# Conditioned residual pair kernel: 8 KB load rows and 16 KB store rows in two rings, and evictions of 2048 columns

## The chip, the cores and the metric

One core of a Trainium2 chip runs the kernel. The metric is the device time of one launch in microseconds (us); the time of a kernel is the median of its runs. Engines are called as the profile calls them: PE is TensorE (PEld its weight loads), DVE is VectorE, ACT is ScalarE, POOL is GpSimd, SP is SyncE. ACTq and SPq are the instruction queues of ACT and SP, from which they issue transfers.

## The reference

```python
def reference(x, itok_B_0_15, itok_B_0_31, L0_cond_weights, L1_cond_weights, L1_cond_biases):
    # x: (128, 128, 2048) f32; conditions: (128,) int32
    W = L0_cond_weights[itok_B_0_15]               # 16 maps of 128x128
    x = x + einsum('bct,bcd->bdt', x, W)
    w = L1_cond_weights[itok_B_0_31]               # 32 maps of 128x128
    b = L1_cond_biases[itok_B_0_31]
    return x + einsum('bct,bcd->bdt', x, w) + transpose(b, (0, 2, 1))
```

For a sample this is (I + W1)(I + W0) applied to a 128x2048 matrix, plus a bias per row. Input and output are 134 MB each.

## The kernel before

The kernel first makes one 128x128 map for each sample, the product of the two maps with the identity added to each, and then multiplies the sample by it. It works on 64 pairs of samples (`PAIRS`), q = 0 to 63.

**Layout.** A pair is 2 MB. It is loaded in one transfer of 128 rows of 16 KB: partition k*64+i holds channels 2i and 2i+1 of sample k of the pair (`x_pairs`, lines 34 on). So sample 0 lies on partitions 0 to 63 and sample 1 on 64 to 127, and u = 0, 1 names the even and the odd channels. There are 8 slots (`xt`, `SLOTS`). The result is written back into the slot it was read from, and stored from there in rows of 16 KB.

**SP** (lines 101 to 110) loads the weights and then the pairs. From the ninth pair on it waits, before it loads into a slot, until the store from that slot has landed (`stored`).

**POOL** (lines 124 to 138) adds the identity to the two maps of each sample (lines 136 and 137), up to two pairs ahead (`map0T`, `map1`).

**PE** (lines 150 to 209). `combine` (line 154) multiplies the maps, in two matmuls of 256 columns for a pair, into the last 512 columns of `acc1`; ACT copies the halves that are wanted into `both`. `term` (line 159) is a matmul of 512 columns that contracts only 64 partitions: the channels of one parity of one sample. Sample 0 goes to `acc0`, sample 1 to `acc1`, each four PSUM banks of 512 columns, and each bank takes two terms (u = 0 and 1). There are 16 terms in a pair, written in turn for the two samples. A float32 matmul is two instructions in the profile (MATMUL x2048 for 1024 terms). Halves of the accumulators (columns 0 to 1023 and 1024 to 2047) are handed over on their own: `lo_done` after the first, `hi_done` after the second.

**DVE** (lines 222 to 233) evicts sample 0 with the bias, four instructions of 64x1024 per pair (lines 224, 226), and **ACT** (lines 242 to 265) sample 1 in the same way (line 251). ACT also copies the combined map of the next pair (lines 246, 247) between its evictions, and issues the pair's store (line 265) once all four parts are out.

The order of PE within a pair is written out by hand (`pair`):

```python
pe.wait_ge(x_loaded[slot], loads)      # then 8 terms on columns 0..1023
pe.wait_ge(hi_out[prev], outs_before)  # the pair before is out of the upper half
combine(next, next_maps)               # then 5 terms on columns 1024..2047
pe.wait_ge(both_ready[next], next_both)
                                       # 2 terms
pe.wait_ge(lo_out[slot], outs)         # last term
```

Eight pairs are unrolled at the start, eight form the body of a loop, and eight are unrolled at the end.

Of the kernel before, what the change touches and what calls it, by code (L numbers as in the profile page):

```python
# [5 lines left out]
def conditioned_residual_kernel(  # L6
# [16 lines left out]
    B, C, T = x.shape  # L23
# [3 lines left out]
    HALF = T // 2  # L27
    SLOTS = 8
    PAIRS = B // 2
    TURNS = PAIRS // SLOTS  # L30
# [4 lines left out]
    x_pairs = x.rearrange("(q k) (i u) t -> q (k i) (u t)", k=2, u=2)  # L35
# [3 lines left out]
    with ctx:  # L39
# [20 lines left out]
        map0T = sb("map0T", [C, 2, 2, 2, HC])  # L60
# [22 lines left out]
        maps_ready = [sem(f"maps_ready{s}") for s in range(SLOTS)]  # L83
        combined = sem("combined")
        both_ready = [sem(f"both_ready{s}") for s in range(SLOTS)]
        lo_done0 = sem("lo_done0")
        lo_done1 = sem("lo_done1")
        hi_done0 = sem("hi_done0")
        hi_done1 = sem("hi_done1")

        lo_out = [sem(f"lo_out{s}") for s in range(SLOTS)]
        hi_out = [sem(f"hi_out{s}") for s in range(SLOTS)]
        x_loaded = [sem(f"x_loaded{q}") for q in range(SLOTS)]
        stored = [sem(f"stored{q}") for q in range(SLOTS)]

        w0T_v = w0T_sb[:, :, :].rearrange("p s (i u) -> p s u i", u=2)
# [5 lines left out]
        @block.sync  # L102
        def _(sp):
            sp.dma_start(w0T_sb[:, :, :], w0T).then_inc(w0_loaded, LOAD)
            sp.dma_start(w1_sb[:, :, :], w1).then_inc(w1_loaded, LOAD)
            for q in range(PAIRS):
                slot = q % SLOTS
                if q >= SLOTS:
                    sp.wait_ge(stored[slot], LOAD * (q // SLOTS))
                sp.dma_start(xt[:, slot, :], x_pairs[q, :, :]).then_inc(x_loaded[slot], LOAD)  # L110

        @block.gpsimd
        def _(pool):
# [9 lines left out]
            GROUP = 16  # L123
            for b in range(B):
                if b % GROUP == 0:
                    _, i0 = nc.values_load_multi_w_load_instructions(  # L126
                        cond_sb[0:1, 0, b:b + GROUP], engines=[POOL], min_val=0, max_val=S0 - 1,
                        skip_runtime_bounds_check_because="conditions index the maps")
                    _, i1 = nc.values_load_multi_w_load_instructions(  # L129
                        cond_sb[0:1, 1, b:b + GROUP], engines=[POOL], min_val=0, max_val=S1 - 1,  # L130
                        skip_runtime_bounds_check_because="conditions index the maps")
# [4 lines left out]
                nc.gpsimd.tensor_tensor(map0T[:, q % 2, :, k, :], w0T_v[:, bass.ds(i0[b % GROUP], 1), :, :], ident_v, ALU.add)  # L136
                nc.gpsimd.tensor_tensor(map1[:, q % 2, k, :, :], w1_v[:, bass.ds(i1[b % GROUP], 1), :, :], ident_v,  # L137
                                        ALU.add).then_inc(maps_ready[q % SLOTS], 1)

        @block.tensor  # L140
        def _(pe):
# [8 lines left out]
            def combine(slot, ready):  # L150

                pe.wait_ge(maps_ready[slot], ready)
                for u in range(2):
                    last = nc.tensor.matmul(acc1[:, CB + u * 2 * C:CB + (u + 1) * 2 * C],  # L154
                                            map0T[:, slot % 2, u, :, :], map1[:, slot % 2, :, :, :], start=True, stop=True)
                last.then_inc(combined, 1)

            def term(acc, k, u, buf, slot, j):
                return nc.tensor.matmul(acc[:, j * CHUNK:(j + 1) * CHUNK], both[k * HC:(k + 1) * HC, buf, u, :],  # L159
                                        xt[k * HC:(k + 1) * HC, slot, u * T + j * CHUNK:u * T + (j + 1) * CHUNK],  # L160
                                        start=u == 0, stop=u == 1)

            def pair(slot, outs, outs_before, next_maps, next_both, loads, begins, ends):

                buf = slot % 2
                prev, next = (slot - 1) % SLOTS, (slot + 1) % SLOTS
                if begins:
                    pe.wait_ge(both_ready[0], 1)

                pe.wait_ge(x_loaded[slot], loads)  # L170
                term(acc0, 0, 0, buf, slot, 0)
                term(acc1, 1, 0, buf, slot, 0)
                term(acc0, 0, 1, buf, slot, 0)
                term(acc1, 1, 1, buf, slot, 0)
                term(acc0, 0, 0, buf, slot, 1)
                term(acc1, 1, 0, buf, slot, 1)
                term(acc0, 0, 1, buf, slot, 1).then_inc(lo_done0, 1)
                term(acc1, 1, 1, buf, slot, 1).then_inc(lo_done1, 1)
                if not begins:
                    pe.wait_ge(hi_out[prev], outs_before)  # L180
                if not ends:
                    combine(next, next_maps)
                term(acc0, 0, 0, buf, slot, 2)
                term(acc1, 1, 0, buf, slot, 2)
                term(acc0, 0, 1, buf, slot, 2)
                term(acc1, 1, 1, buf, slot, 2)
                term(acc0, 0, 0, buf, slot, 3)
                if not ends:

                    pe.wait_ge(both_ready[next], next_both)  # L190
                term(acc1, 1, 0, buf, slot, 3)
                term(acc0, 0, 1, buf, slot, 3).then_inc(hi_done0, 1)
                if not ends:
                    pe.wait_ge(lo_out[slot], outs)
                term(acc1, 1, 1, buf, slot, 3).then_inc(hi_done1, 1)

            def group(twos, twos_before, twos_after, after, now, loads, begins, ends):

                for s in range(SLOTS):
                    wraps = s == SLOTS - 1  # L200
                    pair(s, twos, twos_before if s == 0 else twos, twos_after if wraps else twos,
                         after if wraps else now, loads, begins and s == 0, ends and wraps)

            pe.wait_ge(bias_ready, 1)
            combine(0, 2)
            group(2, 0, 4, 2, 1, LOAD, True, False)
            with pe.Fori(2, TURNS) as now:
                group(now * 2, now * 2 - 2, now * 2 + 2, now + 1, now, now * LOAD, False, False)
            group(2 * TURNS, 2 * TURNS - 2, 2 * TURNS + 2, TURNS + 1, TURNS, TURNS * LOAD, False, True)

        @block.vector
        def _(dve):
# [9 lines left out]
            def even_out(q, a):  # L222

                nc.vector.tensor_scalar(xt[0:HC, q % SLOTS, a:a + HALF], acc0[0:HC, a:a + HALF],  # L224
                                        bias_of[0:HC, 2 * q:2 * q + 1], None, ALU.add)
                return nc.vector.tensor_scalar(xt[0:HC, q % SLOTS, T + a:T + a + HALF], acc0[HC:C, a:a + HALF],  # L226
                                               bias_of[HC:C, 2 * q:2 * q + 1], None, ALU.add)

            for q in range(PAIRS):
                dve.wait_ge(lo_done0, q + 1)  # L230
                even_out(q, 0).then_inc(lo_out[q % SLOTS], 1)
                dve.wait_ge(hi_done0, q + 1)
                even_out(q, HALF).then_inc(hi_out[q % SLOTS], 1)

        @block.scalar
        def _(act):
# [5 lines left out]
            def copy_maps(q):  # L242

                act.wait_ge(combined, q + 1)
                crossed = acc1[:, CB:T].rearrange("p (u k c) -> p u k c", u=2, k=2)
                nc.scalar.activation(both[0:HC, q % 2, :, :], crossed[0:HC, :, 0, :], ACT.Identity)  # L246
                nc.scalar.activation(both[HC:C, q % 2, :, :], crossed[HC:C, :, 1, :], ACT.Identity).then_inc(both_ready[q % SLOTS], 1)  # L247

            def odd_out(q, v, a):

                return nc.scalar.activation(xt[HC:C, q % SLOTS, v * T + a:v * T + a + HALF], acc1[v * HC:(v + 1) * HC, a:a + HALF],  # L251
# [3 lines left out]
            for q in range(PAIRS):  # L255
                act.wait_ge(lo_done1, q + 1)
                odd_out(q, 0, 0)
                if q < PAIRS - 1:
                    copy_maps(q + 1)
                odd_out(q, 1, 0).then_inc(lo_out[q % SLOTS], 1)  # L260
                act.wait_ge(hi_done1, q + 1)
                odd_out(q, 0, HALF)
                odd_out(q, 1, HALF).then_inc(hi_out[q % SLOTS], 1)
                act.wait_ge(hi_out[q % SLOTS], 2 * (q // SLOTS + 1))
                act.dma_start(out_pairs[q, :, :], xt[:, q % SLOTS, :]).then_inc(stored[q % SLOTS], LOAD)
            for q in range(SLOTS):
                act.wait_ge(stored[q], LOAD * TURNS)
# [27 lines left out]
```

## Time and profile before

| what | value |
|---|---|
| median of 3 runs | 642.13 us (642.07 to 642.19) |
| the profiled execution: its own time | 642.29 us |
| its span | 640.4 us |
| PE busy | 538.4 us (84%) |
| DVE busy | 329.2 us (51%) |
| ACT busy | 333.5 us (52%) |
| POOL busy | 124.2 us (19%) |
| moved by DMA | 271.82 MB, mean 424 GB/s |

The span is the time between the first and the last event of the execution; its own time is 1.9 us longer. Shares are of the span. Busy time says how full an engine is on average and not who waits for whom: that is in the waits, the chain that ended last and the timeline. There are 16 DMA engines; a queue's share is the time of its packets over 16 times the span. A packet is one row of a transfer as one engine moves it.

### The profile page before, as it was taken

Reading aid. Unit: us, or ns where it says so; the run is one execution under the profiler, and the core shown is the slowest. Engines: PE = TensorE matmul, PEld = TensorE weight load, DVE = VectorE, ACT = ScalarE, POOL = GpSimd, SP = SyncE. Lnnn points to the kernel's source line nnn. Section 1 sums busy time; section 2 is a strip of 40 time slices with the busy share of each in tenths; the row PEclk is TensorE's granted clock in tenths of the full one; section 3 lists DMA queues with packets and bytes.
Section 4 is the critical chain, followed back from the end, with each engine's and each line's share of the span. In section 5 each row is a group of like instructions: output and inputs, shape, how many; then the busy total and the mean of one; then the engine's idle time right before and its main releaser. Section 6 shows DMA issues by size and latency. Waiting matters only on the chain.

```text
span 640.4 us, 6061 instructions
## 1 busy us (share of the span) xinstructions
PE 538.4 (84%) x2308; PEld 234.3 (37%) x2308; DVE 329.2 (51%) x259; ACT 333.5 (52%) x385; POOL 124.2 (19%) x263
## 2 busy tenths in 40 slices
PE   1899999999889889888898898888988988988860
PEld 0344444444334333333333333333333333433320
DVE  0266666666554455455545554555455445545550
ACT  0366666666555465455554654555555545545550
POOL 2322222222122122121221221211212212112000
PEclk9999999999999999999999999999999999999995
DMA  8999999999999999999999999999999999999996
GB/s 363 433 415 427 431 432 426 431 433 428 432 433 427 432 434 427 431 434 427 432 434 426 433 435 426 432 433 428 433 431 428 433 431 430 431 433 428 434 429 262
DMA packets 18931, 271.82 MB, mean 424 GB/s; under 512 B 2241, under 2 KB 2274, under 8 KB 2274
## 3 DMA queue, kind: packets, MB, share of 16 engines
q1 hardware_dynamic: 9504, 137.37, 50.3%
q10 hardware_dynamic: 9410, 134.26, 49.0%
q8 instruction: 7, 0.11, 0.1%
q14 instruction: 10, 0.08, 0.0%
HBM read 137.40 MB, written 134.22 MB: 424 GB/s over the span
## 4 chain that ended last, share of the span: by engine, by line
DMA 64%; PE 29%; DVE 3%; POOLq 0%; ACT 0%; issue 0%; DVEq 0%; POOL 0%; SPq 0%; ACTq 0%
DMA out_dram<-xt 40%; PE acc L159 25%; DMA xt<-in_x_dram 23%; PE acc L154 4%; DMA w_sb<-in_w_dram 1%; DVE xt L224 1%; DVE xt L226 1%; DVEq L39 0%; ACT L246 0%; POOLq L126 0%; POOLq L129 0%; POOL map0T L136 0%; POOL map L137 0%; ACT both L247 0%; ACT both L246 0%
## 5 line engine op out<-in xcount | busy, mean ns | idle before, releaser
L159 PE MATMUL acc<-xt,both 64*128 64x512 f32 x2048 | 472.5, 603 | 67.9 <-DMA xt<-in_x_dram 65.7
L251 ACT ACTIVATE xt<-acc,bias_of 64x1024 f32<-64x1024 f32 x256 | 283.7, 1108 | 270.1 <-PE acc L159 267.7
L159 PEld LDWEIGHTS acc<-xt,both 64*128 64x128 f32 x2048 | 189.8, 188 | 319.0 <-issue 211.5
L224 DVE TENSOR_SCALAR xt<-acc,bias_of 64x1024 f32<-64x1024 f32 x128 | 163.3, 1276 | 278.2 <-PE acc L159 278.2
L226 DVE TENSOR_SCALAR xt<-acc,bias_of 64x1024 f32<-64x1024 f32 x128 | 165.0, 1289 | 1.9
L136 POOL TENSOR_TENSOR map0T<-w0T_sb,ident 128x128 f32<-128x128 f32 x128 | 65.6, 513 | 465.8 <-PE acc L154 454.0
L154 PE MATMUL acc<-map,map0T 128*128 128x256 f32 x256 | 73.3, 409 | 1.2 <-POOL map L137 1.2
L137 POOL TENSOR_TENSOR map<-w_sb,ident 128x128 f32<-128x128 f32 x128 | 65.7, 513 | 0.0
L154 PEld LDWEIGHTS acc<-map,map0T 128*128 128x128 f32 x256 | 43.9, 191 | 53.0 <-issue 36.7
L247 ACT ACTIVATE both<-acc 64x256 f32<-64x256 f32 x64 | 24.3, 380 | 0.8
L246 ACT ACTIVATE both<-acc 64x256 f32<-64x256 f32 x64 | 24.2, 377 | 0.8
L246 ACT ACT_TABLE_LOAD x1 | 1.3, 1283 | 17.4 <-PE acc L154 17.4
L145 PE MATMUL acc<-ident,bias_sb 128*32 128x128 f32 x2 | 0.6, 418 | 10.8 <-DMA bias_sb<-in_bias_dram 10.8
L215 DVE TENSOR_TENSOR onehot<-cond_rep,row 32x128 f32<-32x128 int32 x1 | 0.3, 279 | 12.6 <-DMA cond_rep<-in_conds_dram 12.6
L145 PEld LDWEIGHTS acc<-ident,bias_sb 128*32 128x32 f32 x2 | 0.2, 142 | 10.8 <-DMA bias_sb<-in_bias_dram 10.8
L148 PE MATMUL acc<-onehot,biasT 32*128 32x128 f32 x2 | 0.8, 481 | 1.9 <-DVE biasT L217 1.9
L148 PEld LDWEIGHTS acc<-onehot,biasT 32*128 32x128 f32 x2 | 0.5, 304 | 2.3 <-DVE onehot L215 2.3
L219 DVE COPY bias_of<-acc 128x128 f32<-128x128 f32 x1 | 0.3, 292 | 0.9 <-PE acc L148 0.9
L217 DVE COPY biasT<-acc 32x128 f32<-32x128 f32 x1 | 0.3, 278 | 0.0
L117 POOL TENSOR_SCALAR_AFFINE_SELECT ident<-ident 128x128 f32<-128x128 f32 x1 | 0.3, 283 | 0.0
L114 POOL MEMSET ident<- 128x128 f32 x1 | 0.2, 204 | 0.3 <-POOLq L284 0.3
L115 POOL IOTA row<- 32x128 int32 x1 | 0.2, 224 | 0.0
(4 smaller groups left out, 0.4 us busy)
## 6 DMA issues: line engine op xcount, KB each, us to landing
xt<-in_x_dram SPq DMA_DIRECT2D x64, 2048.0 KB, 24.5
out_dram<-xt ACTq DMA_DIRECT2D x64, 2048.0 KB, 42.9
w_sb<-in_w_dram SPq DMA_DIRECT2D x1, 2048.0 KB, 9.4
w0T_sb<-in_w0T_dram SPq DMA_DIRECT2D x1, 1024.0 KB, 4.8
cond_sb<-in_conds_dram ACTq DMA_DIRECT2D x1, 1.0 KB
bias_sb<-in_bias_dram ACTq DMA_DIRECT2D x1, 16.0 KB, 9.4
cond_rep<-in_conds_dram ACTq DMA_DIRECT2D x1, 16.0 KB, 10.8
```

Source lines behind the costliest of these rows:

```text
L117: nc.gpsimd.affine_select(out=ident[:, :], in_=ident[:, :], compare_op=ALU.not_equal, fill=1.0, base=0, pattern=[[-1, C]], channel_multipl ...
L136: nc.gpsimd.tensor_tensor(map0T[:, q % 2, :, k, :], w0T_v[:, bass.ds(i0[b % GROUP], 1), :, :], ident_v, ALU.add)
L137: nc.gpsimd.tensor_tensor(map1[:, q % 2, k, :, :], w1_v[:, bass.ds(i1[b % GROUP], 1), :, :], ident_v, ALU.add).then_inc(maps_ready[q % SLO ...
L145: nc.tensor.matmul(acc0[0:S1, 0:C], bias_sb[:, :], ident[:, :], start=True, stop=True).then_inc(turned, 1)
L148: nc.tensor.matmul(acc1[:, 0:B], biasT[:, :, :], onehot[:, :], start=True, stop=True).then_inc(picked, 1)
L154: last = nc.tensor.matmul(acc1[:, CB + u * 2 * C:CB + (u + 1) * 2 * C], map0T[:, slot % 2, u, :, :], map1[:, slot % 2, :, :, :], start=Tru ...
L159: return nc.tensor.matmul(acc[:, j * CHUNK:(j + 1) * CHUNK], both[k * HC:(k + 1) * HC, buf, u, :], xt[k * HC:(k + 1) * HC, slot, u * T + j ...
L224: nc.vector.tensor_scalar(xt[0:HC, q % SLOTS, a:a + HALF], acc0[0:HC, a:a + HALF], bias_of[0:HC, 2 * q:2 * q + 1], None, ALU.add)
L226: return nc.vector.tensor_scalar(xt[0:HC, q % SLOTS, T + a:T + a + HALF], acc0[HC:C, a:a + HALF], bias_of[HC:C, 2 * q:2 * q + 1], None, AL ...
L246: nc.scalar.activation(both[0:HC, q % 2, :, :], crossed[0:HC, :, 0, :], ACT.Identity)
L247: nc.scalar.activation(both[HC:C, q % 2, :, :], crossed[HC:C, :, 1, :], ACT.Identity).then_inc(both_ready[q % SLOTS], 1)
L251: return nc.scalar.activation(xt[HC:C, q % SLOTS, v * T + a:v * T + a + HALF], acc1[v * HC:(v + 1) * HC, a:a + HALF], ACT.Identity, bias=b ...
```

## The change

The sample is no longer folded by parity. A load puts channel c of both samples of a pair on partition c, as two rows of 8 KB (256 rows per pair), into a ring of 6 slots of its own (`xin`). Results go to a second ring of 4 slots (`xout`) in the old folded layout, and stores keep their rows of 16 KB.

- SP waits, before it loads pair q, for `done1` of pair q-6, that is for PE to have read the slot, and no longer for a store.
- A term contracts all 128 partitions, so a pair takes 8 terms and not 16. `combine` multiplies only the two products that are wanted, in two matmuls of 128 columns, and ACT copies them in one instruction of 128x256.
- PE does the four terms of sample 0 (`acc0`), hands over the whole accumulator (`done0`), then combines for the next pair and does the four terms of sample 1 (`done1`).
- DVE and ACT each evict a sample in two instructions of 64x2048.
- PE waits for the store of pair q-4 to have landed before its second term of pair q, and for the load of pair q+1 before the second term of sample 1 of pair q.
- ACT waits for DVE's result before its second eviction of the pair.
- The unrolled groups are of 12, the loop body is of 12 and runs three times, then 12 and 4 more are unrolled.

```diff
-    x_pairs = x.rearrange("(q k) (i u) t -> q (k i) (u t)", k=2, u=2)
+    x_pairs = x.rearrange("(q k) c t -> c q k t", k=2)
     out_pairs = out.rearrange("(q k) (i u) t -> q (k i) (u t)", k=2, u=2)
...
-        xt = sb("xt", [C, SLOTS, 2 * T])
+        xin = sb("xin", [C, IN, 2, T])
+        xout = sb("xout", [C, OUT, 2 * T])
...
-                if q >= SLOTS:
-                    sp.wait_ge(stored[slot], LOAD * (q // SLOTS))
-                sp.dma_start(xt[:, slot, :], x_pairs[q, :, :]).then_inc(x_loaded[slot], LOAD)
+                if q >= IN:
+                    sp.wait_ge(done1, q - IN + 1)
+                sp.dma_start(xin[:, q % IN, :, :], x_pairs[:, q, :, :]).then_inc(x_loaded[q % GROUP], LOAD)
...
+            def combine(k, p):
+                return nc.tensor.matmul(acc1[:, CB + k * C:CB + (k + 1) * C], map0T[:, p % 2, k, :], map1[:, p % 2, k, :, :],
+                                        start=True, stop=True)
+            def term(acc, k, p, j):
+                return nc.tensor.matmul(acc[:, j * CHUNK:(j + 1) * CHUNK], both[:, p % 2, k, :],
+                                        xin[:, p % IN, k, j * CHUNK:(j + 1) * CHUNK], start=True, stop=True)
+            def pair(p, turn_before, turn_after, loads, loads_after, stores, begins, ends):
+                prev, next = (p - 1) % GROUP, (p + 1) % GROUP
+                if begins and p == 0:
+                    pe.wait_ge(both_ready[0], 1)
+                    pe.wait_ge(x_loaded[0], loads)
+                else:
+                    pe.wait_ge(out0[prev], turn_before)
+                term(acc0, 0, p, 0)
+                if not (begins and p < OUT):
+                    pe.wait_ge(stored[(p - OUT) % GROUP], stores)
+                term(acc0, 0, p, 1)
+                if not ends:
+                    pe.wait_ge(maps_ready[next], turn_after)
+                term(acc0, 0, p, 2)
+                term(acc0, 0, p, 3).then_inc(done0, 1)
+                if not (begins and p == 0):
+                    pe.wait_ge(out1[prev], turn_before)
+                if not ends:
+                    combine(0, p + 1)
+                    combine(1, p + 1).then_inc(combined, 1)
+                term(acc1, 1, p, 0)
+                if not ends:
+                    pe.wait_ge(x_loaded[next], loads_after)
+                term(acc1, 1, p, 1)
+                term(acc1, 1, p, 2)
+                if not ends:
+                    pe.wait_ge(both_ready[next], turn_after)
+                term(acc1, 1, p, 3).then_inc(done1, 1)
...
+                dve.wait_ge(done0, q + 1)
+                nc.vector.tensor_scalar(xout[0:HC, q % OUT, 0:T], acc0[0:HC, :], bias_of[0:HC, 2 * q:2 * q + 1], None, ALU.add)
+                nc.vector.tensor_scalar(xout[0:HC, q % OUT, T:2 * T], acc0[HC:C, :], bias_of[HC:C, 2 * q:2 * q + 1], None,
+                                        ALU.add).then_inc(out0[q % GROUP], 1)
...
+                nc.scalar.activation(both[:, q % 2, :, :], acc1[:, CB:CB + 2 * C], ACT.Identity).then_inc(both_ready[q % GROUP], 1)
+            def odd_out(q, v):
+                return nc.scalar.activation(xout[HC:C, q % OUT, v * T:(v + 1) * T], acc1[v * HC:(v + 1) * HC, :],
                                             ACT.Identity, bias=bias_of[v * HC:(v + 1) * HC, 2 * q + 1:2 * q + 2])
...
             for q in range(PAIRS):
                 if q < PAIRS - 1:
                     copy_maps(q + 1)
+                act.wait_ge(done1, q + 1)
+                odd_out(q, 0)
+                act.wait_ge(out0[q % GROUP], q // GROUP + 1)
+                odd_out(q, 1).then_inc(out1[q % GROUP], 1)
+                act.wait_ge(out1[q % GROUP], q // GROUP + 1)
+                act.dma_start(out_pairs[q, :, :], xout[:, q % OUT, :]).then_inc(stored[q % GROUP], LOAD)
```

## Rows read from the trace of the kernel before

**Rows 1.** The page's span in 40 slices: granted PE clock, DMA busy share and rate.
```profile
PEclk9999999999999999999999999999999999999995
DMA  8999999999999999999999999999999999999996
GB/s 363 433 415 427 431 432 426 431 433 428 432 433 427 432 434 427 431 434 427 432 434 426 433 435 426 432 433 428 433 431 428 433 431 430 431 433 428 434 429 262
```

**Rows 2.** The page's DMA queues: packets, MB, share of 16 engines (q1 loads, q10 stores).
```profile
q1 hardware_dynamic: 9504, 137.37, 50.3%
q10 hardware_dynamic: 9410, 134.26, 49.0%
q8 instruction: 7, 0.11, 0.1%
```

**Rows 3.** Waits of SP's queue: us in total, times, longest us.
```profile
SPq L110 <- DMA out_dram<-xt: 563.2, 56, 42.8
```

**Rows 4.** The chain that ended last, in order of time: start us, us, what.
```profile
132.97 7.07 PE acc L159 x32
141.10 7.07 PE acc L159 x32
...
155.50 40.01 DMA out_dram<-xt
195.53 24.59 DMA xt<-in_x_dram
```

**Rows 5.** Timeline of PE, two pairs in mid-span: start us, us, instructions, idle before.
```profile
406.82 3.70 PE L159 MATMUL acc<-xt,both 64*128 64x512 f32 x16 [1.43 <-DMA xt<-in_x_dram]
...
416.62 3.70 PE L159 MATMUL acc<-xt,both 64*128 64x512 f32 x16 [1.40 <-DMA xt<-in_x_dram]
```

**Rows 6.** The page's DMA issues: KB each, median us from issue to landing.
```profile
xt<-in_x_dram SPq DMA_DIRECT2D x64, 2048.0 KB, 24.5
out_dram<-xt ACTq DMA_DIRECT2D x64, 2048.0 KB, 42.9
...
w0T_sb<-in_w0T_dram SPq DMA_DIRECT2D x1, 1024.0 KB, 4.8
...
bias_sb<-in_bias_dram ACTq DMA_DIRECT2D x1, 16.0 KB, 9.4
```

**Rows 7.** End of the timeline: the last pair on PE, and the issue of its store.
```profile
613.06 7.14 PE L159 MATMUL acc<-xt,both 64*128 64x512 f32 x32 [1.41 <-DMA xt<-in_x_dram]
...
622.84 0.34 ACTq L265 DMA_DIRECT2D out_dram<-xt  x1
```

**Rows 8.** DMA queues from 634.7 to 639.4 us: packets, MB, share of 16 engines.
```profile
q10 hardware_dynamic: 10, 0.11, 5.7%
```

**Rows 9.** DMA queue from 3 to 4.2 us, when only rows of 8 KB move.
```profile
q1 hardware_dynamic: 62, 0.51, 100.9%
```

**Rows 10.** DMA queues from 6 to 9 us: 16 KB rows on q1, 128-byte rows on q10.
```profile
q1 hardware_dynamic: 80, 1.31, 101.9%
q10 hardware_dynamic: 80, 0.01, 2.2%
```

**Rows 11.** DMA queue q10 from 10 to 30 us, packets of 512 bytes and less.
```profile
q10 hardware_dynamic: 66, 0.02, 0.4%
```

**Rows 12.** The page's groups: busy us, mean ns of one, idle before and releaser.
```profile
L159 PE MATMUL acc<-xt,both 64*128 64x512 f32 x2048 | 472.5, 603 | 67.9 <-DMA xt<-in_x_dram 65.7
L251 ACT ACTIVATE xt<-acc,bias_of 64x1024 f32<-64x1024 f32 x256 | 283.7, 1108 | 270.1 <-PE acc L159 267.7
...
L224 DVE TENSOR_SCALAR xt<-acc,bias_of 64x1024 f32<-64x1024 f32 x128 | 163.3, 1276 | 278.2 <-PE acc L159 278.2
...
L154 PE MATMUL acc<-map,map0T 128*128 128x256 f32 x256 | 73.3, 409 | 1.2 <-POOL map L137 1.2
...
L247 ACT ACTIVATE both<-acc 64x256 f32<-64x256 f32 x64 | 24.3, 380 | 0.8
...
L219 DVE COPY bias_of<-acc 128x128 f32<-128x128 f32 x1 | 0.3, 292 | 0.9 <-PE acc L148 0.9
```

More of the change, by code:

```diff
@@ L82, in conditioned_residual_kernel @@
         bias_ready = sem("bias_ready")
-        maps_ready = [sem(f"maps_ready{s}") for s in range(SLOTS)]
         combined = sem("combined")
[L85 to L96, printed above, removed]
+        done0 = sem("done0")
+        done1 = sem("done1")
+        x_loaded = [sem(f"x_loaded{p}") for p in range(GROUP)]
+        stored = [sem(f"stored{p}") for p in range(GROUP)]
+        maps_ready = [sem(f"maps_ready{p}") for p in range(GROUP)]
+        both_ready = [sem(f"both_ready{p}") for p in range(GROUP)]
+        out0 = [sem(f"out0_{p}") for p in range(GROUP)]
+        out1 = [sem(f"out1_{p}") for p in range(GROUP)]
         w1_v = w1_sb[:, :, :].rearrange("p s (i u) -> p s u i", u=2)
@@ L148, in _ @@
             nc.tensor.matmul(acc1[:, 0:B], biasT[:, :, :], onehot[:, :], start=True, stop=True).then_inc(picked, 1)
[L150 to L167, printed above, removed]
-                    pe.wait_ge(both_ready[0], 1)
[L170 to L180, printed above, removed]
-                if not ends:
[L182 to L187, printed above, removed]
@@ L188, in pair @@
                 if not ends:
-                    pe.wait_ge(both_ready[next], next_both)
-                term(acc1, 1, 0, buf, slot, 3)
-                term(acc0, 0, 1, buf, slot, 3).then_inc(hi_done0, 1)
+                    combine(0, p + 1)
+                    combine(1, p + 1).then_inc(combined, 1)
+                term(acc1, 1, p, 0)
                 if not ends:
[L194 to L202, printed above, removed]
@@ new lines, in pair, with group @@
+                if not ends:
+                    pe.wait_ge(both_ready[next], turn_after)
+                term(acc1, 1, p, 3).then_inc(done1, 1)
+            def group(places, now, before, after, loads, loads_before, loads_after, begins, ends):
+                for p in range(places):
+                    wraps = p == GROUP - 1
+                    pair(p, before if p == 0 else now, after if wraps else now, loads, loads_after if wraps else loads,
+                         loads_before if p < OUT else loads, begins, ends and p == places - 1)
@@ new lines, in _ @@
+            pe.wait_ge(bias_ready, 1)
+            pe.wait_ge(maps_ready[0], 1)
+            combine(0, 0)
+            combine(1, 0).then_inc(combined, 1)
+            group(GROUP, 1, 0, 2, LOAD, 0, 2 * LOAD, True, False)
+            with pe.Fori(2, FULL) as now:
+                group(GROUP, now, now - 1, now + 1, now * LOAD, now * LOAD - LOAD, now * LOAD + LOAD, False, False)
+            group(GROUP, FULL, FULL - 1, FULL + 1, FULL * LOAD, (FULL - 1) * LOAD, (FULL + 1) * LOAD, False, False)
```

57 lines of the change are left out of this document (16 added, 41 removed).

## The prediction

> **What bounds the kernel now.** I read the slices first. The DMA engines are full from the second slice to the last but one, at about 431 GB/s [rows 1], while TensorE's granted clock is at its upper level (2.4 GHz) up to the last slice. The two queues share that time almost evenly, 50.3% and 49.0%, so packets fill 99.3% of sixteen engines' span [rows 2]. The waits and the chain say the same of the order of work: SP, which only loads, stands for 563.2 us behind stores that have not landed [rows 3]. The chain consists of PE work in the first part, with pairs 8.13 us apart (132.97, 141.10), and from 155 us on it goes round through a store of 40.0 us, a load of 24.6 us and a short piece of compute [rows 4]. In mid-span PE starts pairs 9.80 us apart and each time has waited 1.4 us for the load [rows 5]. So compute is done in 8.1 us and DMA sets 9.8.
>
> The pitch can be taken apart. Sixteen-KB packets take 0.611 us: 101.9% of 16 x 3 us over 80 packets [rows 10]. A pair is 8 such packets per engine to load and 8 to store, 16 x 0.611 = 9.78 us. That is the whole pitch, so the engines are never idle in mid-span.
>
> The end matters too. The last load lands just before 613.06 us, and the span ends 27.3 us later [rows 7]. From 634.7 to 639.4 us the packets fill 5.7% of sixteen engines, 0.91 of one engine: a single engine is about 5 us behind the other fifteen [rows 8]. I take it to be the one that also fetches instructions (7 packets of 16 KB on a queue of their own) [rows 2]. What it still has at 613 us is a backlog of stores: at 42.9 us from issue to landing over a pitch of 9.8, 4.4 stores are under way [rows 5, 6]; about 0.9 of these is already moved, and two more are to come, 5.5 x 8 x 0.611 = 26.9 us of packets. It has that to do and finishes about 1 us before the span ends. So even in the tail the slowest DMA engine never stands idle, and compute of the last pair (9.8 us from 613.06 to its store's issue at 622.84) is hidden under stores. The kernel's time is this engine's packets plus some 3 us. A change can then move the time in only two ways: by the time of the packets, or by opening a hole in the slowest engine's work.
>
> **The packets (paid in full).** Loads go from 8 rows of 16 KB to 16 rows of 8 KB per engine and pair, 64 x 8 = 512 more packets on each engine. The 8 KB rows of the first weights took 100.9% of 16 x 1.2 us over 62 packets, 0.312 us each [rows 9]; two are 0.013 us more than one of 16 KB, 512 x 0.013 = 6.6 us. That window is short and its edges cut packets, so it is the upper end. Another bound: 66 packets of at most 512 bytes took 0.4% of 16 x 20 us, 1.28 us; their 0.02 MB at 27 GB/s per engine are 0.74 us, which leaves 8 ns per packet that no byte explains [rows 11]. That is 512 x 0.008 = 4.1 us. The lower end is nothing: a fixed part might hide under the other queue's packet. I take 4.1 us, which comes from the most packets, in a mixed stretch like the one that counts. The Trainium skill (DMA: Bandwidth & Descriptors, "Why small descriptors are slow") charges each DMA operation 32 bytes of descriptor metadata: 8192 more of them would be 0.26 MB or, as an estimate, 0.6 us, and a sum by it would come 3.5 us lower; rows 11 show more than that per packet.
>
> **How the engines share between the two queues.** From 6 to 9 us, q10 moved 80 packets of about 128 bytes and q1 moved 80 of 16 KB [rows 10]: packets alternate one for one, whatever their size. So a 16 KB bias load took 9.4 us [rows 6]. Now both queues have 16 KB packets and share evenly; after the change a load packet is half as long, so stores get two thirds of an engine whenever both have work. A store of 4.9 us of packets then needs 4.9 / (2/3) = 7.4 us, less than the 9.85 us between stores, and its backlog drains. What piles up are loads: with 6 slots, pair q+6 is issued when q has been read, so four to five loads are always queued and the engines stay busy. Steady pitch: 9.80 + 8 x 0.008 = 9.86 us.
>
> **Compute (hidden).** Eight terms are 16 instructions of 512 columns. Before, 32 such in two concurrent rows take 7.07 us [rows 4], 0.43 us a step, so four terms are 8 x 0.43 = 3.4 us and eight 6.9. Combining goes from four instructions in 1.15 us (73.3/64) to four of half the columns, 0.6 to 1.15 [rows 12]; I take 0.7. DVE: 128 columns take 0.292 us and 1024 take 1.276, so 1.1 ns per column and 2048 take 2.40, two are 4.8 us; ACT: 256 columns 0.380, 1024 columns 1.108, so 2048 take 2.08, two are 4.2 us [rows 12]. (Upper ends: twice the present instruction, 5.1 and 4.4 us.) Two circles limit a pair: 3.4 of sample 0's terms, then DVE's 4.8, together 8.3 with hand-overs; and 4.2 of ACT, 0.7 combine, 3.4 terms, 8.4. Both lie under 9.86 with 1.4 us to spare. The new wait for the next load stands in mid-pair: after it landed (L), PE still does three terms, 2.7 us with fill; ACT evicts until L+6.9; then combine and one term, until L+8.5. That too fits. POOL's additions keep their number and size and wait for PE as now; SP's wait moves to `done1` and has nothing but loads behind it. ACT's wait for DVE holds its second eviction, the store and the next map copy, but DVE is done 4.8 us after sample 0, before sample 1's terms plus one eviction (3.4 + 0.7 + 2.1). PE's wait for the store of four pairs ago comes some 25 us after its issue, against 7.4 us of packets and 2 of latency. None of this is seen while loads are the last to come; if that cover went, each microsecond of pitch over 9.86 would cost up to 64.
>
> **The tail (opened).** Count from L, the landing of the last load. Store 61 was issued at L-9.86+7.0 = L-2.9. From issue to first packet I take 1.2 us and from last packet to landing 1.0: a 1 MB load landed in 4.8 us [rows 6] of which 8 x 0.312 = 2.5 are packets. So store 61 runs from L-1.7, has done 1.1 us of its 4.9 by L, and ends at L+3.8. Store 62 is issued at L+7.0 (2.7 + 4.2 + 0.1), runs from L+8.2 to L+13.1: a hole of 4.4 us. Pair 63's sample 1 starts on PE when ACT has left, L+6.9, takes 3.6 with fill, then ACT 4.2 and 0.1: issue at L+14.8, packets from L+16.0 to L+20.9: a hole of 2.9. The span ends at about L+21.9. Both holes together, 7.3 us, are time in which the slowest engine has nothing, where it now has none. Ends: 5.5 us (faster evictions, quicker first packet) to 9.
>
> **The sum.** 640.4 + 4.1 + 7.3 = 651.8 us of span. The profiled execution took 642.29 for its span of 640.4, and the median of the runs shown is 642.13; added to the median, 642.1 + 11.4 = 653.5 us. At the start nothing moves: six loads fill the engines until about 40 us, and the seventh is issued at about 30.
>
> **Rivals.**
> *Shares go by bytes (0.15), the one that can end on the other side.* If the two queues keep equal halves of the engines, stores drain in 9.8 us, no faster than they come; the backlog built while compute sets the pace (8.4 against 9.8 per pair over some twenty pairs) stays, up to the 25 us that PE's wait for `stored` lets pass. Then 2.3 stores are left at L, 11 us, and no hole opens. Only the packets' term is left: 642.1 + 4.1 = 646.2, from 642.1 to 648.7. It ends as no change or better if the fixed part is under 2.5 ns a packet. Rows 10 speak against it. The Trainium skill (DMA: Bandwidth & Descriptors, "Queues, rings and completion order") has an engine drain a packet of about 9 to 17 descriptors from one ring before it switches; that would be a whole transfer's 16 small rows against 8 large ones, equal bytes, and hence this rival's time. By that rule, rows 10 should have shown runs of packets and not equal counts.
> *The slowest engine is relieved (0.04).* It is 4.7 us behind the rest [rows 8]. If the new code fetched fewer instructions and the backlog also stayed, the time would come to 638 to 641. But the unrolled pairs rise from 24 to 40 while the instructions per pair halve.
> *Compute becomes the bound (0.05).* If evictions of 2048 columns across four banks cost 0.8 us more each than I take, the circle passes 9.86; at 10.2 us per pair it adds some 20 us, 674. PE is less full, 7.6 of 9.86 us; would its clock fall to the lower level, terms would take 13.7 us and the time pass 900. Gaps of 1.4 us leave it high now [rows 1, 5].
> *The two rows of a partition lie 1 MB apart in memory and read slower (0.03).* Each tenth on the loads' packets is 1024 x 0.031 = 32 us.
> *My forecast: 0.73.*
>
> **How the numbers follow.** A measurement of this kernel can tell about 0.2%, 1.3 us. Faster: 0.04 from the relieved engine and 0.02 of the byte shares; same: 0.04 of the byte shares; slower: all else, 0.90. The forecast's own ends are 642.1 + 5.5 = 647.6 and 642.1 + 6.6 + 9 = 657.7. The range reaches down into the byte shares: 645.0 to 657.5.
>
> **What would show it.** Per step: q1 with about 17,700 packets and a share some 0.6 points up; pitch of 9.86 us; stores landing in 10 us and not 42.9, loads in 40 or more; SP waiting for PE; the last load landing about 22 us before the end, and a hole in the rate between L+4 and L+8 and again near L+13 to L+16. It is wrong if stores still take over 25 us to land (shares by bytes), if PE waits longest for DVE or ACT in mid-span (compute bound), or if the pitch is not 9.8 to 9.9.

## The result, and the profile after

The changed kernel takes 647.67 us, the median of 5 runs (647.26 to 649.29), against 642.11 for the kernel before in the same series. The ratio is 1.0087, with a 95% interval of 1.0076 to 1.0098. It is 5.6 us slower. The forecast was slower by 11.4 us, from 645.0 to 657.5. The sign is right and the time lies in the range, but the size was forecast at twice what was measured.

The page of the changed kernel: its span, the slices (clock, DMA share, rate), the queues, and the two large groups of transfers with KB each and median us to landing. They answer to [rows 1, 2, 6].

```profile
span 645.5 us, 3621 instructions
...
PEclk9999999999999999999999999999999999999998
DMA  8999999999999999999999999999999999999986
GB/s 362 428 409 429 429 427 428 429 437 429 423 427 429 429 428 432 432 423 429 430 428 434 430 425 430 429 428 439 424 431 424 426 433 429 425 431 427 427 366 260
...
q1 hardware_dynamic: 17696, 137.37, 50.5%
q10 hardware_dynamic: 9410, 134.26, 48.6%
q8 instruction: 6, 0.10, 0.1%
q14 instruction: 7, 0.06, 0.0%
...
xin<-in_x_dram SPq DMA_DIRECT2D x64, 2048.0 KB, 46.0
out_dram<-xout ACTq DMA_DIRECT2D x64, 2048.0 KB, 11.5
```

DMA still fills the span, but the last slice but one is thinner: 366 GB/s, where there were 429. Stores now land in 11.5 us and not in 42.9, loads in 46.0 and not in 24.5: the queue that used to be long is short, and the other way round.

The page's groups of the changed kernel (busy us, mean ns, idle before) answer to [rows 12].

```profile
L155 PE MATMUL acc<-xin,both 128*128 128x512 f32 x1024 | 469.2, 601 | 84.1 <-DMA xin<-in_x_dram 75.2
L240 ACT ACTIVATE xout<-acc,bias_of 64x2048 f32<-64x2048 f32 x128 | 251.1, 1962 | 287.0 <-PE acc L155 286.2
L222 DVE TENSOR_SCALAR xout<-acc,bias_of 64x2048 f32<-64x2048 f32 x64 | 149.9, 2343 | 320.1 <-PE acc L155 320.1
...
L151 PE MATMUL acc<-map,map0T 128*128 128x128 f32 x256 | 45.2, 300 | 34.6 <-ACT xout L240 32.6
```

Evictions of 2048 columns cost 2.34 us on DVE and 1.96 on ACT (forecast 2.40 and 2.08), combining 45.2/64 = 0.71 us a pair (0.7). PE still waits longest for loads.

The chain that ended last in the changed kernel (start us, us, what) shows the pitch: five pairs lie between two of its PE pieces.

```profile
134.66 2.85 PE acc L155 x6
...
183.68 2.86 PE acc L155 x6
...
232.43 2.85 PE acc L155 x6
...
427.82 2.86 PE acc L155 x6
...
624.13 2.86 PE acc L155 x6
```

From 232.43 to 427.82 are 20 pairs, 9.77 us each; from there to 624.13 another 20, 9.82 each. Forecast was 9.86 throughout, and 9.77 lies outside the 9.8 to 9.9 that were to confirm it. Before the change it was 9.82: from 406.82 [rows 5] to 613.06 [rows 7] are 21 pairs. The 9.80 of the prediction is a single step of it.

The end of the timeline of the changed kernel, from the landing of the last load.

```profile
624.13 6.28 PE L155 MATMUL acc<-xin,both 128*128 128x512 f32 x14 [1.38 <-DMA xin<-in_x_dram]
627.01 3.94 ACT L240 ACTIVATE xout<-acc,bias_of 64x2048 f32<-64x2048 f32 x2 [4.70 <-PE acc L155]
...
630.98 0.34 ACTq L253 DMA_DIRECT2D out_dram<-xout  x1
631.00 3.70 PE L155 MATMUL acc<-xin,both 128*128 128x512 f32 x8 [0.59 <-ACT xout L240]
...
634.74 3.94 ACT L240 ACTIVATE xout<-acc,bias_of 64x2048 f32<-64x2048 f32 x2 [3.79 <-PE acc L155]
638.70 0.34 ACTq L253 DMA_DIRECT2D out_dram<-xout  x1
```

The first line is where PE goes on once the last load has landed. Store 62 is issued 6.9 us after that, store 63 14.6 us after (forecast 7.0 and 14.8), and the span ends 21.4 us after (21.9). The DMA share from 620 to 646 us, in 40 slices of 0.65 us, has the two holes in it:

```profile
DMA  9559999999520000009999999000009999999000
```

By the times of the packets all sixteen engines are idle from 628.5 to 631.8 and from 636.8 to 639.5 us. The order of steps in the tail is as forecast; the first hole is shorter (3.3 us and not 4.4).

The trace also has the start and duration of every packet. It doesn't name a packet's engine, but packets of one engine follow one another end to start. In mid-span one engine started its packets as follows (in ns; the 4-byte packets between, which signal that a transfer is done, are left out):

```
before  16 KB each, queues in turn:  0  607  1214  1821  2429  3036  3643  4250
after   8 KB loads, no store queued: 2  308  613  919  1225
        8 KB and 16 KB in turn:      1531(16)  2138(8)  2444(16)  3051(8)  3357(16)  3964(8)
```

Two things follow. One 16 KB store alternates with one 8 KB load, as the sharing by packets has it. And a packet costs 607.2 ns from start to start at 16 KB and 305.9 at 8 KB: splitting a row costs 4.6 ns, since neighbouring packets overlap by 3 to 4 ns, which their durations (0.611 and 0.309) hide. I had 8 ns.

### The profile page after: what moved, and what is told of

Its sections match the earlier page's. It is cut to its first block, busy times and chain, and to the rows that moved or that the text cites. A ratio compares the mean times of both kernels' runs of the same rounds, so it can differ in the third digit from the quotient of the medians.

```text
span 645.5 us, 3621 instructions
## 1 busy us (share of the span) xinstructions
PE 504.2 (78%) x1284; PEld 215.2 (33%) x1284; DVE 301.6 (47%) x131; ACT 277.0 (43%) x193; POOL 116.4 (18%) x263
## 4 chain that ended last, share of the span: by engine, by line
DMA 86%; PE 9%; ACT 1%; DVE 1%; POOLq 0%; issue 0%; POOL 0%; SPq 0%; DVEq 0%; ACTq 0%
DMA xin<-in_x_dram 85%; PE acc L155 8%; DMA w_sb<-in_w_dram 1%; ACT xout L240 1%; DVE xout L223 1%; DVE xout L222 1%; PE acc L151 0%; ACT L236 0%; POOLq L125 0%; POOLq L128 0%; POOL map0T L135 0%; POOL map L136 0%; ACT both L236 0%; SPq L103 0%; POOLq L135 0%
## 5 line engine op out<-in xcount | busy, mean ns | idle before, releaser
L155 PE MATMUL acc<-xin,both 128*128 128x512 f32 x1024 | 469.2, 601 | 84.1 <-DMA xin<-in_x_dram 75.2
L240 ACT ACTIVATE xout<-acc,bias_of 64x2048 f32<-64x2048 f32 x128 | 251.1, 1962 | 287.0 <-PE acc L155 286.2
L222 DVE TENSOR_SCALAR xout<-acc,bias_of 64x2048 f32<-64x2048 f32 x64 | 149.9, 2343 | 320.1 <-PE acc L155 320.1
L155 PEld LDWEIGHTS acc<-xin,both 128*128 128x128 f32 x1024 | 185.2, 191 | 322.3 <-issue 184.6
L223 DVE TENSOR_SCALAR xout<-acc,bias_of 64x2048 f32<-64x2048 f32 x64 | 150.8, 2356 | 0.9
L135 POOL TENSOR_TENSOR map0T<-w0T_sb,ident 128x128 f32<-128x128 f32 x128 | 58.1, 454 | 487.3 <-PE acc L151 475.6
L151 PE MATMUL acc<-map,map0T 128*128 128x128 f32 x256 | 45.2, 300 | 34.6 <-ACT xout L240 32.6
L151 PEld LDWEIGHTS acc<-map,map0T 128*128 128x128 f32 x256 | 34.4, 192 | 84.3 <-ACT xout L240 79.8
L236 ACT ACTIVATE both<-acc 128x256 f32<-128x256 f32 x64 | 24.6, 384 | 58.3 <-PE acc L151 58.3
## 6 DMA issues: line engine op xcount, KB each, us to landing
out_dram<-xout ACTq DMA_DIRECT2D x64, 2048.0 KB, 11.5
```

The lines of the kernel that those rows point to most:

```text
L135: nc.gpsimd.tensor_tensor(map0T[:, q % 2, k, :], w0T_sb[:, bass.ds(i0[b % BATCH], 1), :], ident[:, :], ALU.add)
L151: return nc.tensor.matmul(acc1[:, CB + k * C:CB + (k + 1) * C], map0T[:, p % 2, k, :], map1[:, p % 2, k, :, :], start=True, stop=True)
L222: nc.vector.tensor_scalar(xout[0:HC, q % OUT, 0:T], acc0[0:HC, :], bias_of[0:HC, 2 * q:2 * q + 1], None, ALU.add)
L223: nc.vector.tensor_scalar(xout[0:HC, q % OUT, T:2 * T], acc0[HC:C, :], bias_of[HC:C, 2 * q:2 * q + 1], None, ALU.add).then_inc(out0[q % GR ...
L236: nc.scalar.activation(both[:, q % 2, :, :], acc1[:, CB:CB + 2 * C], ACT.Identity).then_inc(both_ready[q % GROUP], 1)
L240: return nc.scalar.activation(xout[HC:C, q % OUT, v * T:(v + 1) * T], acc1[v * HC:(v + 1) * HC, :], ACT.Identity, bias=bias_of[v * HC:(v + ...
```

## The experiments

Times are medians; each stands beside runs of the kernel before on the same chip, 642.1 to 642.4 us.

**Stores in rows of 8 KB too.** Is it the ratio of packet sizes that empties the store queue? (The gap of 16 keeps the rows apart.)

```diff
-        xout = sb("xout", [C, OUT, 2 * T])
+        xout = sb("xout", [C, OUT, 2, T + 16])
-                act.dma_start(out_pairs[q, :, :], xout[:, q % OUT, :])
+                act.dma_start(out_pairs[q, :, :, :], xout[:, q % OUT, :, 0:T])
```

> The changed kernel with its stores too in rows of 8 KB, so that packets of both queues have one size. Theory (engines alternate packet for packet): stores lose their two thirds, take over 20 us to land in place of 11.5, a backlog of two to three stores stands at the last load, and the two holes in the tail (about 6 us) close; 512 more packets per engine at 4.6 ns each (start to start 2 x 305.9 against 607.2 ns in the two traces) cost 2.4 us. About 647.5 - 6 + 2.4 = 643.5 to 645 us. Rival (the share does not depend on the packet's size): stores still land in 11 to 12 us, the holes stay, 649 to 650.5 us.

Measured: 644.93 us, 1.0037 of before (1.0027 to 1.0048). With 8192 more packets it is 2.7 us faster than the changed kernel. Its page's transfers:

```profile
xin<-in_x_dram SPq DMA_DIRECT2D x64, 2048.0 KB, 38.4
out_dram<-xout ACTq DMA_DIRECT2D x64, 2048.0 KB, 28.4
```

Stores now take 28.4 us to land. Twice as many small packets make the kernel faster, so it was not their number that cost most, but the unequal shares. Of the two holes one is left, of 1.3 us (635.6 to 636.9).

**Loads in rows of 16 KB.** The same question from the other side: only the load's rows change. Each partition then gets two neighbouring channels of one sample, so this kernel contracts the wrong channels; its amount of work is the same.

```diff
-    x_pairs = x.rearrange("(q k) c t -> c q k t", k=2)
+    x_pairs = x.rearrange("(q k) (i u) t -> q (k i) (u t)", k=2, u=2)
-        xin = sb("xin", [C, IN, 2, T])
+        xin = sb("xin", [C, IN, 2 * T])
```

> The changed kernel with its loads in contiguous rows of 16 KB, everything else as it is. Each partition then holds two neighbouring channels of one sample, so the matmuls contract the wrong rows: the output is not the reference's, the work is the same. Both queues have rows of 16 KB again. Theory (engines alternate packet for packet; a split row costs 4.6 ns): 2.4 us of packets go, and the holes of the tail close as they did with stores of 8 KB (5.1 us): 647.7 - 2.4 - 5.1 = 640.2 us, 639.5 to 641.5, with stores landing in 25 us or more. Rival (the tail belongs to the longer hand-overs and not to the row size): only the packets' part goes, 645 us, stores landing in 12 us.

Measured: 640.85 us, 0.9981 (0.9972 to 0.9991). Its page's transfers:

```profile
xin<-in_x_dram SPq DMA_DIRECT2D x64, 2048.0 KB, 39.7
out_dram<-xout ACTq DMA_DIRECT2D x64, 2048.0 KB, 28.1
```

So the load's row size alone costs 647.67 - 640.85 = 6.8 us. Of these 2.4 are packets (512 x 4.6 ns), which leaves 4.4 for the shares. And everything else in the change is worth 1.4 us: with equal rows it is faster than before.

**The kernel before in rows of 8 KB**, loads and stores, by slots with a gap (`xt` as `[C, SLOTS, 2, T + 16]`). The price of a packet by itself.

> The kernel before with loads and stores in rows of 8 KB (slots padded so that the rows stay apart), nothing else. 1024 more packets per engine. Theory (4.6 ns per packet that is split, nothing else): +4.7 us, 646.8 us, pitch 9.82 + 0.074 = 9.90. Rival (the one engine that is late before is late only with rows of 16 KB): its 4 us go, 642.5 to 643.5 us, pitch 9.82. With 8 ns a packet, as forecast: +8.2 us, 650 us.

Measured: 646.96 us, 1.0069 (1.0048 to 1.0091), +4.6 us: 4.5 ns for each of 1024 packets on an engine. PE starts pairs 9.88 us apart. The 4.6 ns of the packet starts hold, and 8 (650 us) do not.

**Only the rings.** The kernel before with 4 slots for loads and 4 for stores.

```diff
-                if q >= SLOTS:
-                    sp.wait_ge(stored[slot], LOAD * (q // SLOTS))
+                if q >= IN:
+                    sp.wait_ge(hi_done1, q - IN + 1)
```

(DVE and ACT wait for `stored` of pair q-4.)

> The kernel before with two rings (4 slots for loads, 4 for stores), all rows of 16 KB, matmuls, evictions and order as before: a load now waits for PE and not for a store. Open: why the steady pitch of the changed kernel is 9.79 us and not 9.86, where before it was 9.82. Theory A (a load that waits for a store makes one late engine later still): the pitch falls to 9.73 to 9.79, and the time to 639 to 641.5 us. Theory B (it goes with the rows of 16 KB or with the number of instructions): pitch 9.82, 642 us or a little more. Either way stores land in over 20 us, as both queues have rows of one size, and no hole opens.

Measured: 644.84 us, 1.0033 (1.0022 to 1.0044), pitch 9.81. Theory A falls: what a load waits for does not change the pitch. It is 2.5 us slower than the kernel before; single runs of it spread from 643.7 to 645.7. The traces show where time goes: from 27 to 40.5 us its engines move 347 GB/s, and those of the kernel before 409, which is 2.0 us of transfers at 430 GB/s. That fits with fewer slots for loads (4 and not 8) while compute starts up, but no run tests it.

**Stores held back.** Two kernels, both with 5 slots in each ring. The first is that alone (`IN, OUT = 5, 5` and `GROUP = 10`):

> The changed kernel with 5 slots in each ring (groups of 10 instead of 12), as the base of the next one. Four loads fewer one are still queued at any time and stores land long before their slot is needed, so nothing should move: 647 to 648.5 us, 21.4 us from the landing of the last load to the end.

Measured: 647.64 us, 1.008 (1.0063 to 1.0097). The second also issues each store two pairs late, from pair 22 on, and releases those held back around the last load (`store` waits for `out1` of its pair and issues the transfer):

```diff
                 act.wait_ge(done1, q + 1)
+                if HELD_FROM <= q < PAIRS - 1:
+                    store(q - 2 if q < PAIRS - 2 else q - 1)
                 odd_out(q, 0)
...
-                act.wait_ge(out1[q % GROUP], q // GROUP + 1)
-                act.dma_start(out_pairs[q, :, :], xout[:, q % OUT, :]).then_inc(stored[q % GROUP], LOAD)
+                if q < HELD_FROM - 2 or q >= PAIRS - 2:
+                    store(q)
+                elif q == PAIRS - 3:
+                    store(q - 1)
```

> The 5/5 kernel in which, from pair 22 on, a store is issued two pairs late, while loads keep the DMA engines full, and the stores held back are issued one after the other around the last load. Theory (the cost of the change in the tail is that the DMA engines have nothing to do in two holes of 3.3 to 5 and 2.7 to 3 us): the last load lands some 6 us earlier, the engines stay full from there to the end, and the time falls by 6 us against the 5/5 kernel, to 641 to 642 us. Rival (the tail is as long as it is because of the evictions' latency, and the holes only show it): the time stays within 1 us of the 5/5 kernel's.

Measured: 641.68 us, 0.9995 (0.9982 to 1.0008): 6.0 us less than the 5/5 kernel. The DMA share from 620 to 646 us:

```profile
DMA  9999999999999999993199999999000000000000
```

The same packets, in another order, and both holes are gone but for about 1 us. The evictions are the same as in the 5/5 kernel (1.96 and 2.34 us each); what was taken away is idle DMA time. The theory holds and its rival falls.

> The 5/5 kernel with stores held back by two pairs from pair 54 on only (from 22 on in the run before, 641.68 us). The holes are closed in the same way, and less of the span runs with stores late, so the same time or a little less: 640.8 to 641.7 us, 0.1 to 0.2% under the kernel before. If holding back had cost something in mid-span, this gives it back; if the stores held back at the end come too late to fill the holes, 643 us or more.

Held back from pair 54 on only: 642.01 us, 0.9986 (0.9974 to 0.9998), 12 runs from 640.93 to 643.29. That is just above the range expected. Of the kernels here that compute the whole result it is the only one whose interval lies below the kernel before, by 0.1%; from the run before it can't be told apart.

**Instructions beside the work.** The pitch of the changed kernel is below the forecast even with 4.6 ns a packet (9.82 + 8 x 0.0046 = 9.86). Something else had become less. First suspect: the 6061 instructions of the profile, now 3621.

```diff
+                    for n in range(36):
+                        nc.gpsimd.memset(idle_sb[:, q * 36 + n:q * 36 + n + 1], 0)
```

> The changed kernel with 36 one-column memsets on POOL for each pair, 2304 instructions more, all beside other work (POOL is busy 18% of the time). It tells whether one DMA engine is late by the number of instructions that are executed and fetched. If so: some 18 more instruction fetches of 8 KB and a pitch up by 0.05 to 0.1 us, +2 to +6 us. If not: within 1 us of the changed kernel.

Measured: 656.94 us, 1.0223 (1.0202 to 1.0245), 9.3 us more than the changed kernel, where at most 6 were expected. Its page counts 25 packets on q14 where there were 7. Three pairs in its timeline, and q14 from 255.4 to 265 us:

```profile
245.72 6.28 PE L158 MATMUL acc<-xin,both 128*128 128x512 f32 x14 [1.29 <-DMA xin<-in_x_dram]
255.42 6.28 PE L158 MATMUL acc<-xin,both 128*128 128x512 f32 x14 [1.27 <-DMA xin<-in_x_dram]
...
265.83 6.28 PE L158 MATMUL acc<-xin,both 128*128 128x512 f32 x14 [1.97 <-DMA xin<-in_x_dram]
```
```profile
q14 instruction: 1, 0.01, 0.2%
```

Pairs are 9.70 us apart, and 10.41 where a fetch of code falls between; such steps come with every third pair, mostly. Per extra fetch of 8 KB it is 9.3/18 = 0.5 us, more than the 0.31 us of an 8 KB packet. The packets say why: behind each fetch comes a data packet that takes 0.22 to 0.30 us longer than usual (0.53 behind one of them). Execution or fetching? The next kernel tells.

```diff
                 term(acc1, 1, p, 0)
+                for n in range(10):
+                    nc.tensor.matmul(acc1[0:1, CHUNK:CHUNK + 1], ident[:, 0:1], ident[:, 1:2], start=True, stop=True)
```

> The changed kernel with ten one-column float32 matmuls more for each pair (into a column of the accumulator that is overwritten after), where PE waits for the load anyway: about 40 more instructions per pair on PE, as many as the kernel before has more than the changed one (72 against 40). Packets that take 1 to 59 ns too long, all on one DMA engine by their times, sum to 97 ns per pair before and to 52 after the change. Theory (they go with the instructions that PE executes): 90 to 105 ns per pair, the pitch in the second half 9.82, and 1 to 2.5 us more. Rival (they go with the evictions of 1024 columns, or the matmuls on half the rows): 52 ns as in the changed kernel, and within 0.5 us of it apart from code fetches.

Measured: 648.81 us, 1.0105 (1.0088 to 1.0122), 1.1 us more than the changed kernel. It executes 6181 instructions, more than the 5925 of the kernel with memsets, many of them in the loop, and its page has 6 more fetches (12 on q8 against 6). So the number of instructions executed is not what costs 9.3 us. Fetches are what the kernel with memsets has more of, and its steps fall where they do. The six more here, of 16 KB, cost little: the ten matmuls also stand in the tail, where the last store is issued 15.3 us after the last load has landed and not 14.6. That is 0.8 of the 1.1 us, which leaves 0.3 for the six together.

**The packets that take too long.** In all kernels some packets last 1 to 59 ns more than the usual 309 or 611, nearly all of them one behind the other in time, so on one engine. Summed from 170 to 600 us:

```
ns per pair of packets 1 to 59 ns too long
before 97   rings only 88   before in 8 KB rows 90
after  52   stores in 8 KB 47   memsets 56   5/5 rings 44   held back 45 and 43
            PE instructions 45   loads in 16 KB 65
```

They fall with the change, by 45 ns per pair, and neither the rings, the row size nor the number of instructions moves them much.

In four traces the packets' own time (16 x 607.2 ns for rows of 16 KB, 32 x 305.9 for 8 KB, 8 and 16 for the changed kernel) plus this sum gives the time between two pairs:

```
us per pair, stores 17 to 60  packets   too long   sum     measured
before                        9.715     0.10       9.81    9.82
rings only                    9.715     0.09       9.80    9.80
before in 8 KB rows           9.789     0.09       9.88    9.88
after                         9.752     0.05       9.80    9.79
```

So before the change it is this engine that sets the pace. The fetches of code are elsewhere: 14 of the 17 there overlap in time with one of its long packets, so they are on other engines. Nor do pairs come later where a fetch falls, from 171 us on, but for one step of 9.94 us that the next one (9.74) gives back. One fetch of 16 KB is at 548.2 us:

```profile
544.34 3.70 PE L159 MATMUL acc<-xt,both 64*128 64x512 f32 x16 [1.42 <-DMA xt<-in_x_dram]
554.14 3.70 PE L159 MATMUL acc<-xt,both 64*128 64x512 f32 x16 [1.40 <-DMA xt<-in_x_dram]
```

After the change there is one at 237.5 us:

```profile
232.43 6.28 PE L155 MATMUL acc<-xin,both 128*128 128x512 f32 x14 [1.37 <-DMA xin<-in_x_dram]
242.40 6.28 PE L155 MATMUL acc<-xin,both 128*128 128x512 f32 x14 [1.53 <-DMA xin<-in_x_dram]
```

The first step is 9.80 us, as always there; the second is 9.97. From 134.66 to 418 us of the changed kernel three of the 29 steps are such (9.98, 9.97, 9.89, each with a fetch; three more fetches leave no mark), and the other 26 are 9.75 on average, the packets' own time. From 418 us on most are 9.79 to 9.84, with the long packets in them. I read this so: once the long packets had become fewer, an engine with fetches set the pace for the first half, in place of theirs. No experiment tests it.

What makes the packets long? Two candidates were left.

```diff
+                for a in (0, T // 2):
+                    last = nc.scalar.activation(xout[HC:C, q % OUT, v * T + a:v * T + a + T // 2],
+                                                acc1[v * HC:(v + 1) * HC, a:a + T // 2],
+                                                ACT.Identity, bias=bias_of[v * HC:(v + 1) * HC, 2 * q + 1:2 * q + 2])
```

(the same on DVE)

> The changed kernel with each eviction of 2048 columns cut into two of 1024, on DVE and on ACT, no hand-over added. It prices the evictions and tests the last candidate among the instructions for the 52 against 97 ns per pair of packets that take too long. A pair's evictions grow by 2 x 0.2 us on DVE and 2 x 0.25 on ACT. Theory: in mid-span that is hidden (1.4 us of slack), in the tail ACT's 0.5 us counts twice: +1 us, 648.3 to 648.9 us. If the 97 ns go with the number of evictions, they come back and add 1 to 2 us more; if they stay at 45 to 52, they belong to the matmuls on half the rows.

Measured: 648.3 us, 1.0081 (1.0056 to 1.0107), 0.6 us more than the changed kernel, and 49 ns per pair. Evictions are not it. They take 1279 (DVE) and 1101 ns (ACT) each and are hidden in mid-span.

```diff
-                return nc.tensor.matmul(acc[:, j * CHUNK:(j + 1) * CHUNK], both[:, p % 2, k, :],
-                                        xin[:, p % IN, k, j * CHUNK:(j + 1) * CHUNK], start=True, stop=True)
+                return nc.tensor.matmul(acc[:, j * CHUNK:(j + 1) * CHUNK], both[k * HC:(k + 1) * HC, p % 2, k, :],
+                                        xin[k * HC:(k + 1) * HC, p % IN, k, j * CHUNK:(j + 1) * CHUNK], start=True, stop=True)
```

> The changed kernel with its terms contracting 64 partitions and not 128: rows 0 to 63 for sample 0, rows 64 to 127 for sample 1, the other half of each contraction left out. Same number of instructions. It tests the last candidate for the packets that take too long on one DMA engine (52 ns per pair after the change, 97 before; neither PE's instruction count nor the number of evictions brought it back). If matmuls on half the rows do it: 90 ns per pair or more, and up to 1.5 us more. If not: 45 to 52 ns, 647.3 to 648 us, and the cause stays open.

Measured: 765.1 us, 1.1897 (1.1861 to 1.1934), for a reason nobody had expected. Its clock, from the page's slices, and its terms from the groups:

```profile
PEclk9956567676767677676757667676757767676766
...
L155 PE MATMUL acc<-xin,both 64*128 64x512 f32 x1024 | 548.9, 909 | 4.0 <-ACT xout L240 2.2
```

The granted clock is 0.7 on average and goes between its two levels (0.50 from 400 to 402 us, 1.00 from 404 to 408), and PE became the bound. In the changed kernel the same line reads 601 ns and 75.2 us of waiting for loads. Too much else is different in this kernel for its packets to decide anything, so the cause of the 45 ns stays open.

## Why the forecast had the sign and not the size

**Right: what bounds the kernel, and the shares.** Packets of the two queues alternate one for one, so rows of half the size for loads give stores two thirds of an engine. Both kernels that made the rows equal again brought stores back to 28 us; one took all of the cost away, the other, with twice the small packets, about half. The rival of shares by bytes has fallen. So has, for rows of 8 and 16 KB on these two queues, what the Trainium skill says of draining 9 to 17 descriptors at a time (DMA: Bandwidth & Descriptors, "Queues, rings and completion order"): this trace alternates single packets.

**Right: compute is hidden, and how the tail opens.** The two issues came within 0.2 us of the forecast, the edges of the holes within 0.6 and the end of the span within 0.5. The hole term was 7.3 us; the engine that works longest into the first hole has gaps of 3.3 and up to 3.0, 6.3 us. It works 0.6 us longer into it than I reckoned, as it is late (ten of the others stop over 1 us earlier), and the next store's first packet starts 0.85 us after its issue, where I took 1.2. Closing the holes gave 6.0.

**Mis-sized: the packets.** "I take 4.1 us" should have been 512 x 4.6 ns = 2.4. The 8 ns, taken from two figures of one digit, are near a packet's fixed duration (a 4-byte packet takes 9 ns); what counts is start to start, and the kernel before in 8 KB rows measured 4.5. This is 1.7 us of the miss.

**Failed: the step that carried the slowest engine's other work over unchanged.** I counted its packets, wrote "That is the whole pitch", found some 5 us beyond them at the end [rows 8], put these down to the engine that fetches code, and added my two terms to the measured span, as if everything else would stay. With 2.4 and 6.3 us the same sum gives 640.4 + 8.7 = 649.1; the span is 645.5. These 3.6 us are in mid-span: 9.82 + 8 x 0.0046 = 9.86 us a pair would have followed, 9.79 was measured, 0.072 less over the 50 pairs from 134.66 to 624.13.

Packets were not the whole pitch. From start to start 16 of them are 9.715 us and not 9.78; the other 0.10 us are packets that take too long. Two errors cancelled there, and that was luck. The change halved this part: 45 ns a pair, 2.2 us over the 50 pairs. The rest fits with the first half of the span, where the pace was no longer that engine's at all. The fetches are not where I put them: in mid-span before they left no mark, so that there are fewer now (13 on q8 and q14 and not 17) can't have given time back there. This is worked out from the traces and not shown by an experiment, and why the long packets became fewer is open. That the other parts of the change are worth something is shown on its own: with loads of 16 KB it is 1.4 us faster than before. My relieved engine was a rival at 0.04, and only as a whole, where it should have been a term of the sum.

## What to carry to other kernels

When two queues keep the DMA engines full, as here, the one with the smaller packets gets the smaller share, so row sizes decide which queue builds a backlog. A backlog of stores is what hid the last pair's compute here: leave the stores the larger share and the engines run dry at the end; equal rows, or stores held back for the end, close most of the hole. And where the slowest DMA engine is the bound, a term for its other work belongs in the sum. Ask too which engine that is: fetches of unrolled code cost nothing in mid-span before, and 9.3 us in the kernel with memsets, where the engine that fetched was the last.

## What was not expected of the hardware

- In the kernel with memsets most fetches of 8 KB of code made the load in flight land some 0.65 us later (pairs 10.35 to 10.41 us apart and not 9.73), against 0.31 us for an 8 KB data packet: 9.3 us for 18 more of them.
- One of the sixteen engines had packets that took up to 59 ns too long, 97 ns a pair before and 52 after. Before, that set the pace in mid-span.
- Float32 matmuls on 64 of 128 rows, one at a time, had a granted clock of 0.70 on average, with PE busy 80% of the span; with all rows it was 0.996 at 78%, and with two on different halves at once 0.986 at 84% before. The kernels of the first two figures have the same columns and the same count of matmuls, and take 765 us and 648. So the clock does not follow busy time alone.
- Splitting a 16 KB row costs 4.6 ns of an engine, 0.8%, 2.4 us in all; that only one queue had the smaller rows cost nearly twice as much (4.4 us), by its side effect on the tail.
